# Cross-attention with a feed-forward of three blocks: the norm of the first three token blocks in pieces of its own

## The chip, the cores and the metric

The kernel runs on one core of a Trainium2 chip. The metric is the device time of one execution in microseconds (us); less is better.

Engines: PE (TensorE) multiplies matrices and writes to PSUM; DVE (VectorE), ACT (ScalarE) and POOL (GpSimd) work on vectors, POOL on SBUF alone; SP issues the DMAs. Each engine works through its own instructions in order and waits for others by semaphores.

## What is computed

```python
def xattn(KEY, VALUE, QUERY, ...):              # 128 sequences of 64 tokens, D = 128, 16 heads
    k = split_heads(KEY @ Wk.T + bk); q = split_heads(QUERY @ Wq.T + bq); v = split_heads(VALUE @ Wv.T + bv)
    score = einsum('bhij,bhkj->bhik', k, q) / sqrt(dh)
    attn = softmax(score, axis=1)               # over the heads
    out = einsum('bhik,bhij->bhjk', attn, v)
    return merged(out) @ Wo.T + bo

def ffn(x, ...):                                # weights: 4-bit with scales, plus a low-rank part
    h = x
    for blk in range(3):
        y = qlora_linear(h, 2 * blk)
        y = gelu(layernorm(y, gamma[blk], beta[blk]))
        h = qlora_linear(y, 2 * blk + 1) + h
    return h

x = x + xattn(ctx, ctx, layernorm(x), ...)
x = x + ffn(layernorm(x), ...)
```

## The kernel before

The 8192 tokens are 16 chunks of 512 (four tiles of 128 tokens). The first stage is the attention. Each engine has a function `chunk(c, par, half)`, run for c from 0 to 17, with four parts p from 0 to 3; a part handles 128 tokens (one pair of tiles of scores). In a part, with n = 4c + p:

- PE makes the scores of n + 1, adds the shift by the maximum of n, does a share of the projections for later chunks and of the output projection, and multiplies the probabilities of n - 2 by the values.
- DVE takes the negative maximum over the heads of n (`negmax`, L728), then for n - 1 the sum over the heads (`zsum`, L742) and its reciprocal (`rz`, L745). In part 1 it takes the statistics of a later chunk's x (L524); at the end of part 3 it adds the attention's result to x (`x_all`, L749, semaphore `s_x2`).
- ACT takes the exponential of n (L967) and moves results from PSUM to SBUF.
- POOL multiplies the probabilities of n - 1 by `rz` (L476), and in part 1 works out the variance and scale for x of chunk c + 3 (L439 to L445, L426).

The second stage is the feed-forward, a software pipeline over the 16 blocks of 512 tokens. Each engine has a function `step(t, par)`, in which it does what it has to do for block t in the pipeline's first place, for block t - 1 in its second, and so on over eight places. Block t enters with the layer norm of x: on DVE the statistics of x (`input_stats`, L762) and their combination into mean and variance (`combine_input`, L691 to L703); on POOL the scale by a power of -0.5 (L487), the product with the mean (L502), and the scaling and the shift of x into `z[0]` (L506, L511). PE transposes `z[0]` a step later (semaphore `p_z[0]`), ACT moves it into `h[0]`, and PE's first layer of block t - 2 follows. The combination and the power take the statistics of the new block (the first four columns) and those of the first layer of block t - 2 (the last four) in one instruction each. ACT normalises the first layer (`normalise`, L1021) when the power is there (`p_rs[1]`).

Steps 0 to 4 are issued inside the attention, at the ends of the parts that the table `EARLY` names for each engine as (chunk, part); PE's step 3 stands in part 3 of chunk 15, ahead of that part's output projection, and waits for the last exponential (`s_exp`), since it writes into the PSUM of the scores. Steps from 5 on follow the attention. `s_x2` counts the blocks whose x is complete. The order on each engine is the order in which the program issues the instructions; nothing else plans it.

Within a part the order on DVE is negmax of n, statistics, sum and reciprocal of n - 1, the addition to x, and then early steps; on POOL it is the multiply of n - 1, the variance, and then early steps; on ACT the early step of a part comes after that part's exponential and ahead of the next part's.

Of the kernel before, what the change touches and what calls it, by code (L numbers as in the profile page):

```python
# [19 lines left out]
P = 128  # L20
# [33 lines left out]
         "DVE": {0: (12, 3), 1: (13, 3), 2: (15, 1), 3: (16, 0), 4: (16, 3)},  # L54
         "ACT": {0: (12, 3), 1: (13, 3), 2: (15, 2), 3: (15, 3), 4: (16, 2)},
         "POOL": {0: (12, 3), 1: (13, 3), 2: (15, 1), 3: (16, 0), 4: (16, 2)}}
FIRST_STEP = 5


def build(nc, x, ctx_in, wk, bk, wq, bq, wv, bv, wo, bo, qw, qs, qb, la, lb, gamma, beta, out):  # L60
# [8 lines left out]
    with ExitStack() as es:  # L69
# [6 lines left out]
        def sem(name):  # L76
            return es.enter_context(nc.semaphore(name))
# [150 lines left out]
        p_nmr = sem("p_nmr")  # L228
        p_z0 = sem("p_z0_scaled")
# [26 lines left out]
        def early_steps(eng, c, p, step):  # L256

            if isinstance(c, int):
                for t, place in EARLY[eng].items():
                    if place == (c, p):  # L260
                        step(t, t % 2)

# [153 lines left out]
        def _(pool):  # L416
# [49 lines left out]
            def chunk(c, par, half):  # L466
                for p in range(PPC):
                    n = PPC * c + p
                    mc = c - (p == 0)
                    if live(mc):  # L470
                        m = n - 1

                        pool.wait_ge(s_rz, m + 1)
                        e = probs[(p - 1) % 4]
                        by_query = rz[(p - 1) % 4][:, :].unsqueeze(1).unsqueeze(3)
                        nc.gpsimd.tensor_tensor(e[:, :, :, :], e[:, :, :, :],  # L476
                                                by_query.broadcast_to([P, BANDS, SEQ, ADJ]),
                                                ALU.mult).then_inc(s_probs, 1)
                    if p == 1 and live(c + 3):
                        input_variance(c + 3)  # L480
                    early_steps("POOL", c, p, step)


# [6 lines left out]
            def step(t, par):  # L490
                for v, k in ((3, t - 6), (2, t - 4)):
                    if live(k):
                        if some(k):
                            pool.wait_ge(p_z[v], k)
                        norm_scales(v, 0, TPC, k + 1)
                if live(t) or live(t - 2):
                    if live(t - 3):
                        pool.wait_ge(p_z[1], t - 2)
                    norm_scales(1, 0 if live(t) else TPC, 2 * TPC if live(t - 2) else TPC, t + 1)
                if live(t):  # L500
                    pool.wait_ge(p_rs[1], t + 1)
                    nc.gpsimd.tensor_tensor(nmr2[:, :], nm2[:, :], rs2[1][:, 0:TPC], ALU.mult).then_inc(p_nmr, 1)  # L502

                    if some(t - 1):
                        pool.wait_ge(p_zt[0], t - 1)
                    nc.gpsimd.tensor_tensor(z[0][par][:, :, :], x_all[:, t, :, :],  # L506
                                            rs2[1][:, 0:TPC].unsqueeze(2).broadcast_to([P, TPC, D]),
                                            ALU.mult).then_inc(p_z0, 1)
                    pool.wait_ge(p_nmr, t + 1)
                    pool.wait_ge(p_z0, t + 1)  # L510
                    nc.gpsimd.tensor_tensor(z[0][par][:, :, :], z[0][par][:, :, :],  # L511
                                            nmr2[:, :].unsqueeze(2).broadcast_to([P, TPC, D]),
                                            ALU.add).then_inc(p_z[0], 1)
# [7 lines left out]
        def _(dve):  # L521
# [162 lines left out]

            def combine_input(k, lo, hi):

                st, ag = st2[1][:, lo:hi, :], ag2[1][:, :, lo:hi]
                dve.wait_ge(p_bn[1], k + 1)
                if some(k):
                    dve.wait_ge(p_rs[1], k)  # L690
# [4 lines left out]
                dve.wait_ge(p_mv[1], 2 * k + 1)  # L695
                if lo == 0:
                    if some(k):
                        dve.wait_ge(p_nmr, k)
# [3 lines left out]
                dve.wait_ge(p_mv[1], 2 * k + 2)  # L702
# [17 lines left out]
            def chunk(c, par, half):  # L720
                for p in range(PPC):
# [48 lines left out]
            def step(t, par):  # L770
# [18 lines left out]
                if live(t) or live(t - 2):  # L789
                    combine_input(t, 0 if live(t) else TPC, 2 * TPC if live(t - 2) else TPC)  # L790
# [23 lines left out]
        def _(act):  # L814
# [210 lines left out]
            def step(t, par):  # L1025
# [34 lines left out]
                if live(t - 2):  # L1060
                    normalise(1, t - 2, TPC, t + 1, first_layer_bank(1, t, par))
# [403 lines left out]
```

## Time and profile before

| | us |
|---|---|
| median of 3 runs | 375.77 (375.29 to 377.1) |
| the profiled execution | 373.36 |
| its span | 371.6 |

| engine | busy us | share of the span |
|---|---|---|
| PE | 340.4 | 92% |
| DVE | 333.2 | 90% |
| ACT | 285.5 | 77% |
| POOL | 268.6 | 72% |

The span is the time from the first to the last recorded instruction of the profiled execution; the rest of its 373.36 us lies around it. In a timeline row the first number is the start in us from the span's beginning, the second the length, then engine, line and operation, output and inputs with their shapes, and how many instructions are merged; idle time of the engine ahead of it stands in brackets with what ended it. The chain is the work that ended last, followed back from the last instruction. Attention with its early steps runs until about 247 us, the feed-forward alone from there on. The granted clock of TensorE has the mean 0.994.

### The profile page before, as it was taken

The numbers are of one execution on the slowest core, as the hardware profiler recorded it, in microseconds if no ns is written. First come the engines' busy times: TensorE is split into PE (matmuls) and PEld (weight loads), VectorE is DVE, ScalarE is ACT, GpSimd is POOL, SyncE is SP. The second block draws the span as 40 slices with busy tenths as digits, with TensorE's granted clock in tenths as the row PEclk, the third lists the DMA queues.
The fourth block names the chain that finished last, engine by engine and source line by source line (L and its number), as shares of the span: only waits on it lengthen the run. The fifth ranks groups of instructions, "written<-read, shape, count | busy, mean of one in ns | idle before, by whom it ended". The sixth has DMA issues, their size and how long they took to land.

```text
span 371.6 us, 13058 instructions
## 1 busy us (share of the span) xinstructions
PE 340.4 (92%) x4795; PEld 253.4 (68%) x4795; DVE 333.2 (90%) x832; ACT 285.5 (77%) x572; POOL 268.6 (72%) x265
## 2 busy tenths in 40 slices
PE   7777999999999999999979785988999999999983
PEld 5443566677667766776756563775888888888773
DVE  5869999999999999999999999879999999988752
ACT  4585988778888878887867545558899999999862
POOL 4546698788877987788788878867878787873321
PEclk9899999999999999999999999999999999999999
DMA  8784475567548645854661400000010001110112
GB/s 197 217 272 148 143 236 179 157 201 223 174 134 232 202 153 152 254 182 145 185 198 63 140 4 2 3 0 1 2 59 29 28 28 56 31 31 30 57 47 67
DMA packets 54498, 43.29 MB, mean 117 GB/s; under 512 B 4592, under 2 KB 48576, under 8 KB 54464
## 3 DMA queue, kind: packets, MB, share of 16 engines
q1 hardware_dynamic: 53888, 42.31, 37.9%
q10 hardware_dynamic: 576, 0.53, 0.5%
q8 instruction: 21, 0.34, 0.4%
q14 instruction: 13, 0.11, 0.1%
HBM read 26.05 MB, written 16.78 MB: 115 GB/s over the span
## 4 chain that ended last, share of the span: by engine, by line
PE 63%; DVE 23%; issue 6%; ACT 4%; POOL 3%; POOLq 0%; DVEq 0%; ACTq 0%
PE score_ps L1367 10%; DVE negmax L728 7%; DVE zsum L742 7%; PE att_ps L1343 6%; PE score_ps L1281 5%; PE wo_ps L1125 5%; PE work L1428 3%; PE score_ps L1137 3%; PE score_ps L1435 3%; PE work L1161 3%; PE att_ps L1435 3%; PE score_ps L1361 3%; PE work L1167 3%; PE work L1174 2%; DVE st L767 2%
## 5 line engine op out<-in xcount | busy, mean ns | idle before, releaser
L476 POOL TENSOR_TENSOR probs<-probs,rz 128x1024 f32<-128x1024 f32 x64 | 136.3, 2139 | 35.7 <-DVE rz L745 35.5
L487 POOL TENSOR_TENSOR rs<-ve,minus_half 128x4 f32<-128x4 f32 (+1 forms) x50 | 59.3, 1187 | 41.5 <-DVE ve L682 30.1
L967 ACT ACTIVATE probs<-score_ps 128x1024 f32<-128x1024 f32 x64 | 65.7, 1026 | 24.7 <-PE score_ps L1281 24.3
L742 DVE TENSOR_REDUCE zsum<-probs 128x64 f32<-128x1024 f32 x64 | 77.3, 1208 | 0.8 <-ACT probs L967 0.8
L728 DVE TENSOR_REDUCE negmax<-score_ps 128x64 bf16<-128x1024 f32 x64 | 75.2, 1176 | 0.3 <-PE score_ps L1137 0.3
L1021 ACT ACTIVATE z<-score_ps,rs 128x128 f32<-128x128 f32 x160 | 46.0, 383 | 2.6 <-POOL rs L487 2.6
L1367 PEld LDWEIGHTS score_ps<-lin_t,h 128*128 128x128 f32 x320 | 38.9, 191 | 12.1 <-DVE h L805 7.0
L1281 PE MATMUL score_ps<-negmax,ident_bf 128*128 128x512 bf16 x128 | 38.8, 384 | 9.2 <-DVE negmax L728 9.1
L1125 PEld LDWEIGHTS wo_ps<-wo_t,att_t 128*128 128x128 f32 x256 | 36.8, 191 | 13.7 <-issue 12.1
L1367 PE MATMUL score_ps<-lin_t,h 128*128 128x128 f32 x320 | 42.0, 278 | 3.0 <-ACT probs L967 1.1
L1343 PE MATMUL att_ps<-probs,v_diag 128*32 128x64 f32 x2048 | 43.4, 224 | 1.5 <-POOL probs L476 0.7
L1343 PEld LDWEIGHTS att_ps<-probs,v_diag 128*32 128x32 f32 x2048 | 32.8, 108 | 11.4 <-POOL probs L476 3.2
L767 DVE BATCH_NORM_STATS2 st<-score_ps 128x6 f32<-128x128 f32 x160 | 35.6, 286 | 4.2 <-PE score_ps L1367 3.2
L1125 PE MATMUL wo_ps<-wo_t,att_t 128*128 128x128 f32 x256 | 38.2, 275 | 0.0
L745 DVE RECIPROCAL rz<-zsum 128x64 f32<-128x64 f32 x64 | 35.4, 553 | 2.2
L1137 PE MATMUL score_ps<-q_stack,k_stack 64*64 64x128 f16 x1024 | 26.7, 222 | 1.1 <-ACT probs L967 0.5
L1137 PEld LDWEIGHTS score_ps<-q_stack,k_stack 64*64 64x64 f16 x1024 | 16.7, 106 | 12.5 <-issue 11.2
L426 POOL TENSOR_TENSOR half_rstd<-veps,minus_half 128x4 f32<-128x4 f32 x16 | 16.3, 1018 | 11.0 <-DVE veps L536 10.0
L1031 ACT ACTIVATE g<-score_ps,cols 128x512 f32<-128x512 f32 x25 | 19.9, 798 | 5.4 <-PE score_ps L1361 5.4
L1428 PEld LDWEIGHTS work<-lin_t,g 128*128 128x128 f32 x128 | 16.6, 191 | 8.0 <-issue 6.7
L834 ACT ACTIVATE xln<-x_all,half_rstd 128x128 f32 (+1 forms) x60 | 19.1, 393 | 0.4 <-POOL half_rstd L426 0.4
L886 ACT ACTIVATE v_diag<-work 64x512 f32<-64x512 f32 x32 | 18.8, 588 | 0.4
(192 smaller groups left out, 669.7 us busy)
## 6 DMA issues: line engine op xcount, KB each, us to landing
q_parts<-parts SPq DMA_DIRECT2D x15, 512.0 KB, 3.5
k_stack<-k_parts SPq DMA_DIRECT2D x30, 256.0 KB, 3.3
q_stack<-q_parts SPq DMA_DIRECT2D x60, 128.0 KB, 2.9
ctx_sb<-in_ctx SPq DMA_DIRECT2D x16, 256.0 KB, 3.6
k_parts<-parts SPq DMA_DIRECT2D x16, 256.0 KB, 2.8
out<-x_all SPq DMA_DIRECT2D x16, 256.0 KB, 2.3
x_all<-in_x SPq DMA_DIRECT2D x14, 256.0 KB, 3.8
x_all<-in_x SPq DMA_DIRECT2D x1, 512.0 KB, 5.5
```

The lines of the kernel that those rows point to most:

```text
L476: nc.gpsimd.tensor_tensor(e[:, :, :, :], e[:, :, :, :], by_query.broadcast_to([P, BANDS, SEQ, ADJ]), ALU.mult).then_inc(s_probs, 1)
L487: nc.gpsimd.tensor_tensor(rs2[v][:, lo:hi], ve2[v][:, lo:hi], minus_half[:, lo:hi], ALU.pow).then_inc(p_rs[v], 1)
L728: nc.vector.tensor_reduce(negmax[p % 2][:, :], score_ps[p % 2][:, :].rearrange("p (h k) -> p k h", k=SEQ), AX_X, ALU.max, negate=True).the ...
L742: nc.vector.tensor_reduce(zsum[q][:, :], probs[(p - 1) % 4][:, :, :, :].rearrange("p u k s -> p k u s"), AX_XY, ALU.add).then_inc(s_zsum, 1)
L767: ins = nc.vector.bn_stats(st2[v][:, lo + i, :], src[:, TILE * i:TILE * (i + 1)])
L967: nc.scalar.activation(probs[p][:, :, :, :], score_ps[p % 2][:, :].rearrange("p (u s k) -> p u k s", s=ADJ, k=SEQ), ACT.Exp, scale=SCALE). ...
L1021: ins = nc.scalar.activation(z[v][0][:, t, :], src[:, TILE * t:TILE * (t + 1)], ACT.Copy, scale=rs2[v][:, lo + t:lo + t + 1])
L1125: ins = nc.tensor.matmul(wo_ps[:, TILE * t:TILE * (t + 1)], att[:, o, TILE * u:TILE * (u + 1)], wo_t[:, o, b, :], start=False, stop=o == 1 ...
L1137: ins = nc.tensor.matmul(score_ps[mp % 2][SEQ * b:SEQ * (b + 1), c0:c0 + 2 * SEQ], k_stack[mb][half_rows, grp, k0:k0 + SEQ], q_stack[mb][h ...
L1281: ins = nc.tensor.matmul(score_ps[p % 2][:, CHUNK * o:CHUNK * (o + 1)], ident_bf[:, :], negmax[p % 2][:, :].unsqueeze(1).broadcast_to([P, ...
L1343: ins = nc.tensor.matmul(att_ps[32 * grp:32 * (grp + 1), c0:c0 + SEQ], v_diag[mb][:, v0:v0 + 32], probs[mp][:, band(hd), :, hd % ADJ], sta ...
L1367: ins = nc.tensor.matmul(dst[:, TILE * t:TILE * (t + 1)], hk[:, TILE * t:TILE * (t + 1)], lin_t[:, 2 * v - 2, :], start=v == 1 and t == 0, ...
```

## The change

The norm of x for blocks 0, 1 and 2 is taken out of the steps and cut into five pieces, each with a table of places in chunks 12 to 15: statistics and combination on DVE, scale (with the product), scaling and shift on POOL. They have semaphores of their own (`p_xbn`, `p_xmv`, `p_xst`, `p_xrs`). Steps 0 and 1 are gone from DVE and POOL, and step 0 from ACT, since nothing else was in them. Step 2 keeps what it does for the first layer of block 0; on POOL it moves from (15, 1) to (15, 2). Blocks from 3 on are as before, with counts that start later.

```diff
 EARLY = {"PE": {0: (12, 3), 1: (13, 3), 2: (15, 0), 4: (16, 2)},
-         "DVE": {0: (12, 3), 1: (13, 3), 2: (15, 1), 3: (16, 0), 4: (16, 3)},
-         "ACT": {0: (12, 3), 1: (13, 3), 2: (15, 2), 3: (15, 3), 4: (16, 2)},
-         "POOL": {0: (12, 3), 1: (13, 3), 2: (15, 1), 3: (16, 0), 4: (16, 2)}}
+         "DVE": {2: (15, 1), 3: (16, 0), 4: (16, 3)},
+         "ACT": {1: (13, 3), 2: (15, 2), 3: (15, 3), 4: (16, 2)},
+         "POOL": {2: (15, 2), 3: (16, 0), 4: (16, 2)}}
 FIRST_STEP = 5
+
+AHEAD = 3
+X_STATS = {0: (12, 0), 1: (13, 0), 2: (14, 0)}
+X_COMBINE = {0: (12, 2), 1: (13, 2), 2: (14, 2)}
+X_SCALES = {0: (12, 3), 1: (13, 3), 2: (14, 3)}
+X_SCALED = {0: (13, 0), 1: (14, 0), 2: (15, 0)}
+X_SHIFTED = {0: (13, 2), 1: (14, 1), 2: (15, 1)}
...
+        def later(t):
+
+            return not isinstance(t, int) or AHEAD <= t < NCHUNK
...
                     if p == 1 and live(c + 3):
                         input_variance(c + 3)
+                    input_part(X_SCALES, c, p, input_scales)
+                    input_part(X_SCALED, c, p, input_scaled)
+                    input_part(X_SHIFTED, c, p, input_shifted)
                     early_steps("POOL", c, p, step)
 
+            def input_scales(t):
+                pool.wait_ge(p_xst, t + 1)
+                nc.gpsimd.tensor_tensor(rs2[1][:, 0:TPC], ve2[1][:, 0:TPC], minus_half[:, 0:TPC],
+                                        ALU.pow).then_inc(p_xrs, 1)
+                pool.wait_ge(p_xrs, t + 1)
+                input_offset(t)
...
-                if live(t) or live(t - 2):
+                own = later(t)
+                if own or live(t - 2):
                     if live(t - 3):
                         pool.wait_ge(p_z[1], t - 2)
-                    norm_scales(1, 0 if live(t) else TPC, 2 * TPC if live(t - 2) else TPC, t + 1)
-                if live(t):
-                    pool.wait_ge(p_rs[1], t + 1)
...
+                    norm_scales(1, 0 if own else TPC, 2 * TPC if live(t - 2) else TPC, t - 1)
+                if own:
+                    pool.wait_ge(p_rs[1], t - 1)
+                    input_offset(t)
+                    input_scaled(t, par)
+                    input_shifted(t, par)
...
+            def input_stats_ahead(t):
+                dve.wait_ge(s_x2, t + 1)
+                if t > 0:
+                    dve.wait_ge(p_xst, t)
+                input_stats(t).then_inc(p_xbn, 1)
+
+            def combine_ahead(t):
+                st, ag = st2[1][:, 0:TPC, :], ag2[1][:, :, 0:TPC]
+                dve.wait_ge(p_xbn, t + 1)
+                nc.vector.scalar_tensor_tensor(ag[:, 1, :], st[:, :, 2], EPS * D, st[:, :, 5], ALU.add, ALU.add)
+                nc.vector.tensor_tensor(ag[:, 0, :], st[:, :, 1], st[:, :, 4], ALU.add)
+                nc.vector.tensor_tensor(ag[:, 2, :], st[:, :, 1], st[:, :, 4], ALU.subtract).then_inc(p_xmv, 1)
+                dve.wait_ge(p_xmv, 2 * t + 1)
+                if t > 0:
+                    dve.wait_ge(p_nmr, t)
+                nc.vector.tensor_scalar(nm2[:, :], ag[:, 0, :], -0.5, None, ALU.mult)
+                nc.vector.scalar_tensor_tensor(ag[:, 3, :], ag[:, 2, :], 0.25, ag[:, 2, :], ALU.mult,
+                                               ALU.mult).then_inc(p_xmv, 1)
+                dve.wait_ge(p_xmv, 2 * t + 2)
+                nc.vector.scalar_tensor_tensor(ve2[1][:, 0:TPC], ag[:, 1, :], 1.0 / D, ag[:, 3, :], ALU.mult,
+                                               ALU.add).then_inc(p_xst, 1)
...
+                    input_part(X_STATS, c, p, input_stats_ahead)
+                    input_part(X_COMBINE, c, p, combine_ahead)
                     early_steps("DVE", c, p, step)
...
-                if live(t) and isinstance(t, int) and t <= FIRST_STEP:
-                    ins = input_stats(t)
-                    if t < 2:
-                        ins.then_inc(p_bn[1], 1)
+                if isinstance(t, int) and AHEAD <= t <= FIRST_STEP:
+                    input_stats(t)
...
-                if live(t) or live(t - 2):
-                    combine_input(t, 0 if live(t) else TPC, 2 * TPC if live(t - 2) else TPC)
+                if live(t - 2):
+                    combine_input(t, 0 if later(t) else TPC, 2 * TPC)
...
                 if live(t - 2):
-                    normalise(1, t - 2, TPC, t + 1, first_layer_bank(1, t, par))
+                    normalise(1, t - 2, TPC, t - 1, first_layer_bank(1, t, par))
```

`input_scaled` and `input_shifted` hold the two instructions of L506 and L511 with their waits, `input_offset` that of L502, and `input_part` issues a piece at the place in its table.

## Rows read from the trace of the kernel before

**Rows 1.** Busy time in a stretch: us, then each engine, clock, DMA share, GB/s.

```profile
176.58:226.59 50.01, 43.32 (x890) 31.41 (x888) 49.21 (x84) 31.80 (x48) 40.71 (x30) 1.00 0.35 109
```

**Rows 2.** The chain in order of time (start, length, what), chunk 15's end.

```profile
229.45 1.17 DVE negmax L728
...
231.31 1.03 ACT probs L967
...
232.39 1.16 PE score_ps L1367 x8
```

**Rows 3.** Timeline of DVE, chunk 12 and step 0.

```profile
180.50 0.86 DVE L524 BATCH_NORM_STATS2 stats<-x_all 128x6 f32<-128x128 f32 x4
181.27 1.21 DVE L742 TENSOR_REDUCE zsum<-probs 128x64 f32<-128x1024 f32 x1
...
189.14 0.86 DVE L762 BATCH_NORM_STATS2 st<-x_all 128x6 f32<-128x128 f32 x4
190.04 1.69 DVE L691 SCALAR_TENSOR_TENSOR ag<-st 128x4 f32<-128x4 f32 x1
191.65 0.15 DVE L693 TENSOR_TENSOR ag<-st 128x4 f32<-128x4 f32 x1
...
192.26 1.22 DVE L728 TENSOR_REDUCE negmax<-score_ps 128x64 bf16<-128x1024 f32 x1
```

**Rows 4.** Timeline of POOL, chunks 12 to 15.

```profile
183.14 2.14 POOL L476 TENSOR_TENSOR probs<-probs,rz 128x1024 f32<-128x1024 f32 x1 [1.41 <-DVE rz L745]
...
187.48 4.23 POOL L476 TENSOR_TENSOR probs<-probs,rz 128x1024 f32<-128x1024 f32 x2
...
193.66 1.04 POOL L506 TENSOR_TENSOR z<-x_all,rs 128x512 f32<-128x512 f32 x1
194.84 1.04 POOL L511 TENSOR_TENSOR z<-z,nmr 128x512 f32<-128x512 f32 x1
...
200.85 2.13 POOL L476 TENSOR_TENSOR probs<-probs,rz 128x1024 f32<-128x1024 f32 x1 [0.65 <-DVE rz L745]
203.64 2.14 POOL L476 TENSOR_TENSOR probs<-probs,rz 128x1024 f32<-128x1024 f32 x1 [0.65 <-DVE rz L745]
...
223.88 2.13 POOL L476 TENSOR_TENSOR probs<-probs,rz 128x1024 f32<-128x1024 f32 x1 [0.65 <-DVE rz L745]
226.75 1.65 POOL L487 TENSOR_TENSOR rs<-ve,minus_half 128x8 f32<-128x8 f32 x1 [0.74 <-DVE ve L703]
```

**Rows 5.** Timeline of DVE, steps 1 and 2.

```profile
200.69 1.16 DVE L728 TENSOR_REDUCE negmax<-score_ps 128x64 bf16<-128x1024 f32 x1
...
204.02 0.86 DVE L762 BATCH_NORM_STATS2 st<-x_all 128x6 f32<-128x128 f32 x4
204.91 0.89 DVE L691 SCALAR_TENSOR_TENSOR ag<-st 128x4 f32<-128x4 f32 x1
...
206.34 1.22 DVE L728 TENSOR_REDUCE negmax<-score_ps 128x64 bf16<-128x1024 f32 x1
...
223.72 0.81 DVE L762 BATCH_NORM_STATS2 st<-x_all 128x6 f32<-128x128 f32 x4
...
225.36 0.69 DVE L691 SCALAR_TENSOR_TENSOR ag<-st 128x8 f32<-128x8 f32 x1
...
226.59 1.22 DVE L728 TENSOR_REDUCE negmax<-score_ps 128x64 bf16<-128x1024 f32 x1
```

**Rows 6.** Timeline of ACT, step 2: the first layer of block 0 normalised.

```profile
230.01 1.15 ACT L1021 ACTIVATE z<-work,rs 128x128 f32<-128x128 f32 x4
```

**Rows 7.** Timelines of POOL and DVE in the feed-forward: a power and a combine.

```profile
256.06 1.02 POOL L487 TENSOR_TENSOR rs<-ve,minus_half 128x4 f32<-128x4 f32 x1 [0.38 <-DVE ve L682]
...
256.82 0.17 DVE L679 SCALAR_TENSOR_TENSOR ag<-st 128x4 f32<-128x4 f32 x1
```

**Rows 8.** POOL's memsets by line (min/median/max ns); DVE's timeline beside the longest.

```profile
L452 POOL MEMSET v_diag<- x8: 519/524/1206, 16.9 to 23.0; 128x512 f32 x8
...
17.64 0.53 DVE L622 TENSOR_SCALAR w_deq<-qw_in 128x768 f32<-128x768 int32 x1
```

More of the change, by code:

```diff
@@ L261, in early_steps, with input_part @@
                         step(t, t % 2)
+        def input_part(places, c, p, part):
+            if isinstance(c, int):
+                for t, place in places.items():
+                    if place == (c, p):
+                        part(t)
+        def later(t):
+            return not isinstance(t, int) or AHEAD <= t < NCHUNK
         def chunks(eng, body):
@@ L480, in chunk, with input_offset, input_scaled, input_shifted @@
                         input_variance(c + 3)
+                    input_part(X_SCALES, c, p, input_scales)
+                    input_part(X_SCALED, c, p, input_scaled)
+                    input_part(X_SHIFTED, c, p, input_shifted)
                     early_steps("POOL", c, p, step)
+            def input_scales(t):
[4 more added lines that the diff above has]
+                input_offset(t)
+            def input_offset(t):
+                nc.gpsimd.tensor_tensor(nmr2[:, :], nm2[:, :], rs2[1][:, 0:TPC], ALU.mult).then_inc(p_nmr, 1)
+            def input_scaled(t, par=None):
+                if some(t - 1):
+                    pool.wait_ge(p_zt[0], t - 1)
+                nc.gpsimd.tensor_tensor(z[0][t % 2 if par is None else par][:, :, :], x_all[:, t, :, :],
+                                        rs2[1][:, 0:TPC].unsqueeze(2).broadcast_to([P, TPC, D]),
+                                        ALU.mult).then_inc(p_z0, 1)
+            def input_shifted(t, par=None):
+                zt = z[0][t % 2 if par is None else par][:, :, :]
+                pool.wait_ge(p_nmr, t + 1)
+                pool.wait_ge(p_z0, t + 1)
+                nc.gpsimd.tensor_tensor(zt, zt, nmr2[:, :].unsqueeze(2).broadcast_to([P, TPC, D]),
+                                        ALU.add).then_inc(p_z[0], 1)
             def norm_scales(v, lo, hi, count):
@@ L683, in combine_layer @@
                                                ALU.add).then_inc(p_st[v], 1)
+            def input_stats_ahead(t):
[18 more added lines that the diff above has]
+                                               ALU.add).then_inc(p_xst, 1)
             def combine_input(k, lo, hi):
                 st, ag = st2[1][:, lo:hi, :], ag2[1][:, :, lo:hi]
-                dve.wait_ge(p_bn[1], k + 1)
-                if some(k):
-                    dve.wait_ge(p_rs[1], k)
+                dve.wait_ge(p_bn[1], k - 1)
+                if some(k - 2):
+                    dve.wait_ge(p_rs[1], k - 2)
                 nc.vector.scalar_tensor_tensor(ag[:, 1, :], st[:, :, 2], EPS * D, st[:, :, 5], ALU.add, ALU.add)
@@ L694, in combine_input @@
                 nc.vector.tensor_tensor(ag[:, 2, :], st[:, :, 1], st[:, :, 4], ALU.subtract).then_inc(p_mv[1], 1)
-                dve.wait_ge(p_mv[1], 2 * k + 1)
+                dve.wait_ge(p_mv[1], 2 * k - 3)
                 if lo == 0:
-                    if some(k):
-                        dve.wait_ge(p_nmr, k)
+                    dve.wait_ge(p_nmr, k)
                     nc.vector.tensor_scalar(nm2[:, :], ag[:, 0, 0:TPC], -0.5, None, ALU.mult)
```

14 lines of the change are left out of this document (2 added, 12 removed).

## The prediction

> **What bounds the kernel now.** The places that the change touches lie in chunks 12 to 15, so I read the busy time of that stretch first [rows 1]. From the first negmax of chunk 12 to the third of chunk 15 VectorE (DVE) is busy 49.21 of 50.01 us; PE has 43.32, ACT 31.80, GpSimd (POOL) 40.71. Next the chain in order of time [rows 2]: through this stretch it runs on DVE alone (negmax, sum, reciprocal, part after part), leaves it at the last negmax of chunk 15 (229.45), and goes over PE's shift to ACT's last exponential (231.31) and PE's step 3 (232.39). Two things follow. Until 229.45 a microsecond of DVE more or less is a microsecond of the end. At 231.31 the engine to watch is ACT: what delays the last exponential delays everything, because step 3 on PE waits for it and all later PE work stands behind step 3.
>
> Then the timelines of DVE and POOL side by side. At the end of chunk 12 the first instruction of the combine (L691, `ag<-st`, two inputs in SBUF) takes 1.69 us on 4 columns [rows 3]; the same kind of instruction elsewhere takes 0.17 [rows 7]. It ends at 191.73, when POOL's two multiplies of probs (187.48 + 4.23 = 191.71) end [rows 4]. At step 1 it takes 0.89 and ends at 205.80, POOL's multiply at 205.78; at step 2 it takes 0.69 and ends at 226.05, the multiply at 226.01 [rows 4, 5]. Three of three: a DVE instruction with two SBUF inputs waits until the POOL multiply that is under way is done. These waits are 1.52, 0.72 and 0.52 us, together 2.76, and lie on the chain.
>
> **What the change removes from DVE.** Step 0 (189.14 to 192.26, 3.12 us), step 1 (204.02 to 206.34, 2.32) and step 2 (223.72 to 226.59, 2.87), in all 8.31 us, waits included [rows 3, 5].
>
> **What it adds to DVE.** Three times four statistics after parts (12,0), (13,0), (14,0): 0.77 each by the same instruction on x in chunk 12 (180.50 to 181.27), 2.31. Three combines after (12,2), (13,2), (14,2): without a wait 0.71 each (0.61 from the second instruction to the next negmax, 191.65 to 192.26, and some 0.10 for the first), 2.13 [rows 3]. Step 2 keeps the statistics of the first layer (223.72 to 225.36 less 0.77, 0.87) and four of the six combine instructions, an estimated 0.53 as two of the six (0.08 to 0.09 each) go: 1.40 [rows 5]. Sum 5.84. So the third negmax of chunk 15, at 226.59 before, comes 8.31 - 5.84 = 2.47 us earlier, plus the waits for POOL at the new places. Stats lose nothing: one SBUF input, and the old ones ran beside POOL's work at their normal length.
>
> **The waits at the new places.** All three combines now stand right behind a reciprocal, and that reciprocal is what POOL's multiply waits for: DVE's next instruction began at 200.69, the multiply at 200.85, 0.16 us later [rows 4, 5]. The six instructions come as three, a semaphore, two, a semaphore, one. The multiply (2.14 us) thus arrives among them.
> - Chunk 12: POOL is in the variance of chunk 15 then (its next multiply waits from 183.14 + 2.1 to 187.48 behind six small instructions and moves with the statistics added) [rows 4]. Bounds 0 and 0.5 us, taken 0.2, since the small instructions are short and the power doesn't hold DVE up: L679 ran 0.17 us at 256.82 in the middle of a power from 256.06 to 257.08 [rows 7].
> - Chunk 13: DVE's first three get through (0.33 us), the other three stand behind the multiply until about 2.3 us after the combine's start: 2.05 us. `input_shifted` of block 0 (1.04 us, as the row at 194.84) follows the multiply without a gap, and DVE's last instruction, behind its own semaphore, may meet it too: 2.75. Taken 2.4. Lower bound 0, if DVE is through before the multiply reads.
> - Chunk 14: a multiply and the shift of block 1 take 2.14 + 1.04 = 3.18 us, more than a part of DVE (226.59 to 229.45, 2.86), so the shift is still running when the combine starts, by some 0.55 us; the next multiply follows at once. 0.55 + 2.05 = 2.6, lower bound 0.55.
> - Step 2 in (15,1): its combine starts 0.9 us after the reciprocal. POOL has scale 2 (a power, 1.02 [rows 7], and a small product) and scaled 2 (1.04) in the parts before and begins its multiply some 0.5 us late; the wait is 1.8, or 2.8 with the shift of block 2 behind it. Taken 2.3 [rows 4].
>
> Sum 0.2 + 2.4 + 2.6 + 2.3 = 7.5 us in place of a gain: the third negmax of chunk 15 comes 7.5 - 2.47 = 5.0 us later.
>
> The Trainium skill, "SBUF — State Buffer", section "Who interferes with whom", states the rule behind these waits and speaks against the change: a DVE instruction with two SBUF inputs contends with a GpSimd instruction that reads SBUF, one of them blocks fully for the other's whole length, and issue order decides which. It counts `tensor_scalar` in its two-port mode in too, which no row here shows. The multiply's rows agree; the power's row (0.17 us beside a power of 1.02) doesn't. Taken to the letter for the power, chunk 12's combine could wait 1 us more, and the sum would be 6.0 instead of 5.0.
>
> **The wait that is new on ACT.** POOL's step 2 moves from (15,1) to (15,2), behind that part's multiply, while ACT's step 2 stays at (15,2), ahead of the last exponential. It normalises block 0 and needs POOL's power. Before, the power started at 226.75, 0.16 us after the negmax behind the combine [rows 4, 5], and ACT normalised from 230.01 to 231.16 without waiting for it [rows 6]. Now the multiply waits for the reciprocal of (15,2), 2.94 us behind the negmax at S (part 2.86 [rows 2, 5] and 0.08); multiply at S + 3.0 to 5.15, power 1.02 [rows 7] to S + 6.1, normalise 1.15 to S + 7.3, and only then the last exponential. Before, it began at 231.31 = S + 4.72 [rows 2]. That is 2.6 us. Queued behind the waiting instruction are that exponential and, through it, PE's step 3, the output projection of chunk 14 and DVE's last sum. Nothing covers it: the exponential is on the chain.
>
> **The rest.** POOL's pieces replace the same instructions and POOL waits less, but it isn't on the chain. PE's transposes of blocks 0, 1 and 2 find them ready: shift 0 ends 1.04 us after a multiply that ended at 202.98 [rows 4], while PE used it first after the end of chunk 13. ACT's other steps and SP's queue are untouched; no DMA moves. Behind step 3 the order is as before and PE is next in line, so I let nothing be won back.
>
> Sum: + 5.0 + 2.6 = + 7.6 us. The profiled run took 373.36 us (span 371.6 and 1.8 around it), 2.4 below the median of 375.77; a shift of this stretch carries over unchanged, so 375.77 + 7.6 = 383.4.
>
> **Rivals.**
> 1. DVE keeps the port through its six instructions, and waits only where POOL is already reading. For: the longest memset of POOL, 1206 ns against 524, ran while DVE's L622 began, so POOL too can be the one that waits [rows 8]. Against: between DVE's groups stand two semaphores. Waits 0.2 + 0 + 0.55 + 1.8 = 2.55, + 0.1 + 2.6: 378.5.
> 2. Not slower: DVE isn't held up at any of the four places, the mechanism of rival 1 to its end, with POOL's reads always coming last. Price - 2.47 + 0.2 + 2.6 = + 0.3: 376.1. It decides if the six are through before the multiply's first read, that is if this comes over 0.6 us after its start. Against it: the three waits of before.
> 3. The wait of ACT lies beside another wait of the same length (PE's step 3 held by something else), the port as in the forecast: + 5.0, 380.8. Nothing in the chain shows such a wait.
> 4. Faster: rivals 2 and 3 together, - 2.3: 373.5.
> 5. The change doesn't do what it says: the pieces relieve nobody, since POOL's waits in steps 0 and 1 are off the chain and DVE has the same instructions elsewhere. With no other wait that ends at rival 2's time.
>
> **How the numbers follow.** Forecast 0.58 (its own range, by the bounds of the waits, 382.0 to 385.2), rival 1 0.19, rivals 2 and 5 0.11, rival 3 0.06, rival 4 0.06. A measurement of this kernel can tell about 0.5%, 1.9 us, from no change: below 373.9 lies rival 4 (0.06), between 373.9 and 377.7 rivals 2 and 5 and a little of rival 1 (0.13), above it the rest (0.81). The range for 8 in 10 must take in rival 1: 377.4 to 385.2.
>
> **What will show it.** Right: in the combines ahead of (13,3) and (14,3) one instruction of 2 us that ends with a POOL multiply; a gap on ACT ahead of the normalise of block 0, released by POOL's power; the last exponential about 7 us later. Wrong: combine instructions of 0.17 us throughout with multiplies that start later or last longer (rivals 1, 2), or an exponential that is late while PE's step 3 isn't (rival 3).

## The result and the profile after

| | median of 4 runs, us | lowest to highest |
|---|---|---|
| before, on the same chip | 376.44 | 375.29 to 378.37 |
| after | 384.75 | 384.14 to 386.73 |

The ratio is 1.0225 with the interval 1.0188 to 1.0262: the change makes the kernel slower by 8.3 us, where 7.6 were forecast. The profiled execution of after took 385.16 us (span 383.4). That of before, 373.36 us, is among the fastest that before has: its mean granted clock was 0.994, and of the 41 other executions of before that stand beside the experiments one has 0.994 (373.29 us) and forty have 0.976 to 0.990 (373.45 to 378.48 us). Ratios and medians are of the fast runs alone, those within 1.5% of a kernel's fastest; this leaves out three of the ten runs of experiment 3 (380.38 to 381.83 us; its median with them is 377.73) and one of the twelve of experiment 8 (552.79 us at a mean clock of 0.559; with it 371.78).

The stretch of [rows 1], from the first negmax of chunk 12 to the third of chunk 15, is now 55.03 us long instead of 50.01, and DVE is busy in 53.88 of it (us; PE, weight loads, DVE, ACT, POOL; granted clock; DMA share; GB/s):

```profile
179.21:234.24 55.03, 45.11 (x890) 32.79 (x888) 53.88 (x89) 31.75 (x48) 43.77 (x34) 0.97 0.31 99
```

What it is busy with are the combines. They stand in the timeline of DVE of after (start, length, engine, line, operation; L732 to L742 are the combine ahead of its step, L751 to L762 that of step 2, L787 the negmax behind it), in chunks 12, 13, 14 and in step 2:

```profile
189.17 0.10 DVE L732 SCALAR_TENSOR_TENSOR ag<-st 128x4 f32<-128x4 f32 x1
...
189.81 1.23 DVE L787 TENSOR_REDUCE negmax<-score_ps 128x64 bf16<-128x1024 f32 x1
...
202.39 0.10 DVE L732 SCALAR_TENSOR_TENSOR ag<-st 128x4 f32<-128x4 f32 x1
...
202.67 2.04 DVE L738 TENSOR_SCALAR nm<-ag 128x4 f32<-128x4 f32 x1
204.63 0.15 DVE L739 SCALAR_TENSOR_TENSOR ag<-ag 128x4 f32<-128x4 f32 x1
204.81 0.89 DVE L742 SCALAR_TENSOR_TENSOR ve<-ag 128x4 f32<-128x4 f32 x1
205.62 1.21 DVE L787 TENSOR_REDUCE negmax<-score_ps 128x64 bf16<-128x1024 f32 x1
...
218.20 0.53 DVE L732 SCALAR_TENSOR_TENSOR ag<-st 128x4 f32<-128x4 f32 x1
...
218.73 2.08 DVE L734 TENSOR_TENSOR ag<-st 128x4 f32<-128x4 f32 x1
...
221.20 1.23 DVE L787 TENSOR_REDUCE negmax<-score_ps 128x64 bf16<-128x1024 f32 x1
...
231.65 1.47 DVE L751 SCALAR_TENSOR_TENSOR ag<-st 128x4 f32<-128x4 f32 x1
...
233.23 0.89 DVE L759 SCALAR_TENSOR_TENSOR ag<-ag 128x4 f32<-128x4 f32 x1
...
234.24 1.22 DVE L787 TENSOR_REDUCE negmax<-score_ps 128x64 bf16<-128x1024 f32 x1
```

And POOL at the same times, with its multiply (L495), its shift of x (L527) and its power (L533):

```profile
202.56 2.13 POOL L495 TENSOR_TENSOR probs<-probs,rz 128x1024 f32<-128x1024 f32 x1 [0.64 <-DVE rz L804]
204.65 1.04 POOL L527 TENSOR_TENSOR z<-z,nmr 128x512 f32<-128x512 f32 x1
...
217.67 1.04 POOL L527 TENSOR_TENSOR z<-z,nmr 128x512 f32<-128x512 f32 x1
218.67 2.13 POOL L495 TENSOR_TENSOR probs<-probs,rz 128x1024 f32<-128x1024 f32 x1
...
230.96 2.15 POOL L495 TENSOR_TENSOR probs<-probs,rz 128x1024 f32<-128x1024 f32 x1 [0.21 <-DVE rz L804]
233.05 1.05 POOL L527 TENSOR_TENSOR z<-z,nmr 128x512 f32<-128x512 f32 x1
237.25 2.12 POOL L495 TENSOR_TENSOR probs<-probs,rz 128x1024 f32<-128x1024 f32 x1 [3.15 <-DVE rz L804]
239.34 1.01 POOL L533 TENSOR_TENSOR rs<-ve,minus_half 128x4 f32<-128x4 f32 x1
```

These answer [rows 3 to 5]. Each long DVE instruction on four columns ends with a POOL instruction: L738 at 204.71 with the multiply that ends at 204.69, L742 at 205.70 with the shift that ends at 205.69, L734 at 220.81 with the multiply that ends at 220.80. A combine without a wait takes 0.64 us (chunk 12, 189.17 to 189.81). What the others take beyond that is their wait: 3.23 - 0.64 = 2.59 us in chunk 13 and 3.00 - 0.64 = 2.36 in chunk 14. Step 2's four instructions take 2.59 instead of the estimated 0.53: 2.06. Together 7.0. In what follows, "the port" is short for what these rows show: one of the two engines, DVE with its operands in SBUF or POOL, stands until the other's instruction is done.

Next ACT at the end of chunk 15, which answers [rows 6] and the exponential of [rows 2] (L1080 normalises block 0, L1026 is the exponential):

```profile
236.16 1.02 ACT L1026 ACTIVATE probs<-score_ps 128x1024 f32<-128x1024 f32 x1 [3.02 <-PE score_ps L1340]
...
240.39 1.14 ACT L1080 ACTIVATE z<-work,rs 128x128 f32<-128x128 f32 x4 [2.62 <-POOL rs L533]
241.40 1.04 ACT L1026 ACTIVATE probs<-score_ps 128x1024 f32<-128x1024 f32 x1
```

ACT stands still for 2.62 us until POOL's power is through, and the last exponential comes behind it. The chain of waits of after shows the same (start, length, what):

```profile
237.25 2.12 POOL probs L495
239.38 0.98 POOL rs L533
...
241.53 0.92 ACT probs L1026
...
242.49 2.07 PE score_ps L1426 x8
```

Its last line was not foreseen. Before, these matmuls of step 3 took 1.16 us [rows 2]. PE's timeline and the busy time by stretch of after:

```profile
235.52 0.60 PE L1340 MATMUL score_ps<-negmax,ident_bf 128*128 128x512 bf16 x2 [2.47 <-DVE negmax L787]
...
242.49 2.07 PE L1426 MATMUL score_ps<-lin_t,h 128*128 128x128 f32 x8 [3.15 <-ACT probs L1026]
244.36 1.06 PE L1420 MATMUL score_ps<-ident,z 128*128 128x128 f32 x4
```

```profile
218.80:222.48 3.68, 0.02 (x4) 0.01 (x1) 3.61 (x7) 0.00 (x0) 1.99 (x1) 1.00 0.00 0
222.48:227.00 4.52, 4.52 (x48) 3.73 (x48) 4.45 (x6) 2.21 (x3) 2.78 (x2) 0.62 0.00 0
234.24:242.49 8.25, 3.03 (x40) 1.62 (x40) 6.22 (x9) 3.69 (x8) 5.19 (x3) 0.64 0.01 2
242.49:247.60 5.11, 5.09 (x19) 4.06 (x20) 4.52 (x16) 2.52 (x3) 2.44 (x2) 0.57 0.00 2
```

and the stretches of before from its third negmax of chunk 15 to its last exponential, and of step 3:

```profile
226.59:231.31 4.72, 2.26 (x40) 1.34 (x40) 4.68 (x6) 2.64 (x6) 4.33 (x5) 1.00 0.01 3
232.39:236.00 3.61, 3.18 (x19) 2.37 (x20) 3.58 (x11) 2.52 (x3) 3.61 (x3) 1.00 0.00 0
```

Before, step 3 had the clock at 1.00. After, PE was busy for 3.03 of the 8.25 us ahead of step 3, the granted clock fell to a mean of 0.64, and step 3 ran at 0.57, most of it at the lower of the two levels (1.2 of 2.4 GHz). Cut into half microseconds, the clock is 1.00 until 236.5 and 0.50 from 237.0 to 246.5. So it fell a good microsecond after PE had come back from a pause of 2.47 us (233.05 to 235.52), and before ACT's wait for POOL began (237.76). The same happened once more, in chunk 15: PE idled 3.66 us behind chunk 14's combine, and the clock of the 4.5 us after that was 0.62.

For the comparison of kernels I cut the profiled executions at four rows that each of them has: DVE's addition to x of block 9 (the end of chunk 11), the third negmax of chunk 15 (S), the start of the last exponential, and DVE's addition of block 15. A, B and C are the stretches between them. This leaves out the start of the kernel: there after took 2.6 us more than before (from its third negmax to its fourth 7.20 us, 4.69 before), with the same instructions. The traces of the experiments show either length: this first row lies at 175.77 to 176.03 in before and experiments 2 and 4, at 177.60 to 179.82 in the others. In after the clock of that stretch (28.2 to 33.3) was 0.67, before's 1.00, and a DVE tensor_scalar on two columns (L705, 36.37 to 37.41) stood behind a POOL multiply (35.26 to 37.38).

| kernel | A: to S | B: S to the last exponential | C: to the last addition | sum |
|---|---|---|---|---|
| before | 176.03 to 226.59: 50.56 | to 231.31: 4.72 | to 246.50: 15.19 | 70.47 |
| after | 178.66 to 234.24: 55.58 | to 241.40: 7.16 | to 258.04: 16.64 | 79.38 |
| difference | +5.02 | +2.44 | +1.45 | +8.91 |

The profiled difference of 8.91 us in the stretch stands beside 8.31 by the medians; the whole profiled executions differ by 11.8. Since before's profile has a higher clock than nearly all its other executions, C's +1.45 is measured against a good case of before, and is likely less against its median execution.

### The profile page after: what moved, and what is told of

Its sections match the earlier page's. It is cut to its first block, busy times and chain, and to the rows that moved or that the text cites. A ratio compares the mean times of both kernels' runs of the same rounds, so it can differ in the third digit from the quotient of the medians.

```text
span 383.4 us, 13055 instructions
## 1 busy us (share of the span) xinstructions
PE 346.6 (90%) x4795; PEld 257.9 (67%) x4795; DVE 338.4 (88%) x836; ACT 284.7 (74%) x572; POOL 268.5 (70%) x266
## 4 chain that ended last, share of the span: by engine, by line
PE 64%; DVE 22%; issue 5%; POOL 4%; ACT 4%; POOLq 0%; DVEq 0%; ACTq 0%
PE score_ps L1426 10%; PE att_ps L1402 6%; DVE zsum L801 6%; PE score_ps L1340 6%; DVE negmax L787 5%; PE wo_ps L1184 5%; PE score_ps L1196 3%; PE work L1487 3%; PE score_ps L1494 3%; PE work L1220 3%; PE att_ps L1494 3%; PE score_ps L1420 3%; PE work L1226 3%; PE work L1233 3%; POOL probs L495 2%
## 5 line engine op out<-in xcount | busy, mean ns | idle before, releaser
L495 POOL TENSOR_TENSOR probs<-probs,rz 128x1024 f32<-128x1024 f32 x64 | 136.3, 2138 | 47.3 <-DVE rz L804 47.3
L1026 ACT ACTIVATE probs<-score_ps 128x1024 f32<-128x1024 f32 x64 | 65.6, 1025 | 29.1 <-PE score_ps L1340 28.7
L533 POOL TENSOR_TENSOR rs<-ve,minus_half 128x4 f32<-128x4 f32 (+1 forms) x48 | 56.6, 1180 | 42.0 <-DVE ve L720 32.8
L787 DVE TENSOR_REDUCE negmax<-score_ps 128x64 bf16<-128x1024 f32 x64 | 75.6, 1181 | 0.0
L1340 PE MATMUL score_ps<-negmax,ident_bf 128*128 128x512 bf16 x128 | 39.6, 392 | 11.9 <-DVE negmax L787 11.8
L1080 ACT ACTIVATE z<-score_ps,rs 128x128 f32<-128x128 f32 x160 | 45.8, 382 | 2.4 <-POOL rs L533 2.4
L1426 PE MATMUL score_ps<-lin_t,h 128*128 128x128 f32 x320 | 42.9, 282 | 5.1 <-ACT probs L1026 3.1
L1340 PEld LDWEIGHTS score_ps<-negmax,ident_bf 128*128 128x128 bf16 x128 | 7.3, 97 | 18.4 <-DVE negmax L787 13.4
```

What stands on the lines that cost most here:

```text
L495: nc.gpsimd.tensor_tensor(e[:, :, :, :], e[:, :, :, :], by_query.broadcast_to([P, BANDS, SEQ, ADJ]), ALU.mult).then_inc(s_probs, 1)
L533: nc.gpsimd.tensor_tensor(rs2[v][:, lo:hi], ve2[v][:, lo:hi], minus_half[:, lo:hi], ALU.pow).then_inc(p_rs[v], 1)
L787: nc.vector.tensor_reduce(negmax[p % 2][:, :], score_ps[p % 2][:, :].rearrange("p (h k) -> p k h", k=SEQ), AX_X, ALU.max, negate=True).the ...
L1026: nc.scalar.activation(probs[p][:, :, :, :], score_ps[p % 2][:, :].rearrange("p (u s k) -> p u k s", s=ADJ, k=SEQ), ACT.Exp, scale=SCALE). ...
L1080: ins = nc.scalar.activation(z[v][0][:, t, :], src[:, TILE * t:TILE * (t + 1)], ACT.Copy, scale=rs2[v][:, lo + t:lo + t + 1])
L1340: ins = nc.tensor.matmul(score_ps[p % 2][:, CHUNK * o:CHUNK * (o + 1)], ident_bf[:, :], negmax[p % 2][:, :].unsqueeze(1).broadcast_to([P, ...
```

## The experiments

The theory: A's excess is DVE behind POOL at the port, B's is POOL's power behind a multiply, and C's is the clock, which falls because PE is lightly busy while A and B last. The rivals: A is mere length (DVE has its instructions in worse places), B's exponential is late for another reason, and the clock falls whatever ACT waits for. The results in one table, with the cuts of above; ratios are to before's runs on the same chip (medians 375.7 beside the first four, 376.9 beside five and six, 376.56 beside the last two) and are not quotients of the medians. A to C come from one trace each:

| kernel | A | B | C | sum | median us | ratio (interval) |
|---|---|---|---|---|---|---|
| 1 after, POOL's step 2 early | 56.92 | 4.72 | 16.16 | 77.80 | 382.92 | 1.0182 (1.0096 to 1.0269) |
| 2 after, combine ahead of rz | 50.83 | 7.18 | 17.24 | 75.25 | 380.22 | 1.0149 (1.0065 to 1.0233) |
| 3 both | 51.26 | 4.72 | 16.16 | 72.14 | 376.95 | 1.0019 (0.9967 to 1.0071) |
| 4 before, POOL's step 2 late | 51.84 | 7.80 | 16.62 | 76.26 | 380.55 | 1.0151 (1.0069 to 1.0233) |
| 5 = 3, no waits for the port | 47.83 | 4.64 | 16.19 | 68.66 | 373.82 | 0.9897 (0.9847 to 0.9948) |
| 6 after, 70 matmuls of zeros | 56.09 | 7.18 | 17.88 | 81.15 | 383.96 | 1.0194 (1.0140 to 1.0248) |
| 7 after, 38 matmuls of zeros | 55.44 | 7.17 | 15.01 | 77.62 | 381.37 | 1.0133 (1.0061 to 1.0204) |
| 8 = 5, 16 matmuls of zeros | 47.84 | 4.64 | 15.28 | 67.76 | 371.25 | 0.9881 (0.9843 to 0.9920) |

### 1. POOL's step 2 back where it was

```diff
-         "POOL": {2: (15, 2), 3: (16, 0), 4: (16, 2)}}
+         "POOL": {2: (15, 1), 3: (16, 0), 4: (16, 2)}}
```

> The changed kernel with one entry put back: POOL's step 2 at (15,1) instead of (15,2). My theory (the new wait on ACT is real and on the chain): POOL's power of step 2 starts within 0.3 us of DVE's combine, ACT normalises block 0 without a wait, the last exponential starts 4.7 us after the third negmax of chunk 15 instead of 7.2; PE stands idle ahead of its step 3 for about 1 us instead of 3.15, so its clock stays at 2.4 GHz and the matmuls of step 3 take 1.16 us instead of 2.07. The four waits of DVE for POOL stay (about 7 us). Time about 4 us under the changed kernel's 384.75: 380.7, ratio to before 1.011. Rival (the wait lies beside another of the same length): 384.7, ratio 1.022. Rival (the wait goes, but the clock falls all the same): 382.3.

B is 4.72 again, to the hundredth that of before, and ACT's last exponential waits for PE's shift and no longer for POOL. But step 3 isn't at full clock (timelines of ACT and PE, then its stretch):

```profile
241.46 1.02 ACT L1026 ACTIVATE probs<-score_ps 128x1024 f32<-128x1024 f32 x1 [0.16 <-PE score_ps L1340]
...
242.53 1.45 PE L1426 MATMUL score_ps<-lin_t,h 128*128 128x128 f32 x8 [1.11 <-ACT probs L1026]
```

```profile
242.50:247.30 4.80, 4.75 (x19) 3.53 (x20) 4.70 (x16) 2.55 (x3) 4.26 (x2) 0.64 0.00 0
```

The wait of ACT is shown as the cause of B, whole. Of C only 0.48 us came back, and the median, 382.92, lies by the case in which the clock falls all the same. The 2.44 us of ACT's wait are therefore not needed for it to fall. A was 1.34 us longer than after's, 0.87 of it in chunk 15 and 0.49 in chunk 14: PE's clock was low for longer there and DVE waited for it. The gain stands on the rows more than on the medians: the interval of the ratio overlaps that of after.

### 2. The combine ahead of the reciprocal

```diff
                                                 AX_XY, ALU.add).then_inc(s_zsum, 1)
+                        input_part(X_COMBINE, c, p, combine_ahead)
                         dve.wait_ge(s_zsum, m + 1)
                         nc.vector.reciprocal(rz[(p - 1) % 4][:, :], zsum[q][:, :]).then_inc(s_rz, 1)
...
-                    input_part(X_COMBINE, c, p, combine_ahead)
```

The six instructions are the same; only the one that releases POOL's multiply now comes after them.

> The changed kernel with the three combines put between DVE's sum and its reciprocal instead of behind the reciprocal, so that POOL's multiply, which waits for that reciprocal, can't start among their six instructions. My theory (a DVE instruction with its operands in SBUF stands behind a POOL instruction that is under way): the wait in chunk 13 (2.59 us) goes to under 0.1, the one in chunk 14 falls from 2.36 to about 1.0, since the shift of block 1 is still running there, step 2 keeps its 2.1, ACT keeps its wait and PE its low clock at step 3. About 4.3 us under the changed kernel: 380.4, ratio 1.011. Rival (the waits only move to POOL, which then makes DVE or PE late elsewhere): 384, ratio 1.02. Rival (the instruction is slow for another reason than POOL, as its place behind a reciprocal): the same 2 us instructions at the new place in both chunks or in neither.

DVE's timeline, chunks 13 and 14 and step 2:

```profile
199.27 0.17 DVE L738 TENSOR_SCALAR nm<-ag 128x4 f32<-128x4 f32 x1
...
212.08 1.04 DVE L733 TENSOR_TENSOR ag<-st 128x4 f32<-128x4 f32 x1
...
223.85 1.78 DVE L751 SCALAR_TENSOR_TENSOR ag<-st 128x4 f32<-128x4 f32 x1
...
225.74 0.89 DVE L759 SCALAR_TENSOR_TENSOR ag<-ag 128x4 f32<-128x4 f32 x1
```

L738 takes 0.17 us where it took 2.04. In chunk 14 what is left is the shift of block 1, which waits for no reciprocal (212.07 to 213.10 on POOL); step 2 was not moved and waits as before. A falls by 4.75 us, B is as in after. So A is the port, and the place of six small instructions by half a microsecond decides over some 4 us. That A was mere length is refuted: the same instructions are there. So is that a place behind a reciprocal makes them slow: chunk 12's combine stood behind one in after and took 0.64 us, and L733 here stands ahead of one and took 1.04. The intervals of the two ratios just overlap, but every run (379.41 to 382.23 us) is below after's fastest (384.14).

### 3. Both

> Both edits together: combines ahead of the reciprocal, POOL's step 2 at (15,1). If the two causes are separate and both on the chain, their gains add: 384.75 - 4.0 - 4.3 = 376.4, ratio to before 1.000. If they share time (one is hidden when the other is gone), clearly less than the sum: 379 or more.

376.95 (376.4 were expected if the gains add), ratio 1.0019: the change as it stands with these two edits undoes the loss, to what can be told. In the stretch the gains were 1.58 and 4.13 alone and 7.24 together; 0.91 us of the 1.53 beyond the sum of the two is in A, where experiment 1 had met the low clock for longer, the rest in C.

### 4. The kernel before with one entry moved

```diff
-         "POOL": {0: (12, 3), 1: (13, 3), 2: (15, 1), 3: (16, 0), 4: (16, 2)}}
+         "POOL": {0: (12, 3), 1: (13, 3), 2: (15, 2), 3: (16, 0), 4: (16, 2)}}
```

> The kernel before with one entry changed: POOL's step 2 at (15,2) instead of (15,1), nothing else. It does the one part of the change alone. There the step also holds block 2's own norm, so the power has 8 columns (1.65 us). My theory: the last exponential starts about 3 us later behind the third negmax of chunk 15 than before (4.72), and PE idles long enough ahead of step 3 for its clock to fall: 3 to 5 us over before, 379.5 to 381.5, ratio 1.008 to 1.013. Rival (hidden): 376.4, ratio 1.000.

Timelines of ACT and PE, and the stretch of step 3:

```profile
234.40 1.14 ACT L1021 ACTIVATE z<-work,rs 128x128 f32<-128x128 f32 x4 [3.26 <-POOL rs L487]
...
236.50 2.07 PE L1367 MATMUL score_ps<-lin_t,h 128*128 128x128 f32 x8 [4.21 <-ACT probs L967]
```

```profile
236.40:241.70 5.30, 5.18 (x19) 4.17 (x20) 5.02 (x16) 2.60 (x4) 4.58 (x3) 0.58 0.01 2
```

This is ACT's wait alone, with nothing of the five pieces: B +3.08 (POOL's power is here on eight columns and takes 1.65 us, not 1.01), and C +1.43 at a clock of 0.58. One entry in a table costs 4.85 us by the medians. A was also longer by 1.28 us; it lies in chunk 13, where the instructions are those of before and DVE waited for ACT and PE at a lower clock:

```profile
190.00:204.00 14.00, 11.94 (x227) 8.05 (x225) 12.88 (x17) 8.38 (x15) 11.04 (x8) 0.88 0.36 114
```

Before had 1.00 there. Why it fell in this execution and not in that of before is open.

### 5. No wait for the port at all

Experiment 3 with DVE's step 2 moved ahead of the reciprocal of (15, 1), the shift of block 1 a part later, and POOL's shifts behind its early steps:

```diff
-         "DVE": {2: (15, 1), 3: (16, 0), 4: (16, 3)},
+         "DVE": {3: (16, 0), 4: (16, 3)},
...
-X_SHIFTED = {0: (13, 2), 1: (14, 1), 2: (15, 1)}
+X_SHIFTED = {0: (13, 2), 1: (14, 2), 2: (15, 1)}
...
-                    input_part(X_SHIFTED, c, p, input_shifted)
                     early_steps("POOL", c, p, step)
+                    input_part(X_SHIFTED, c, p, input_shifted)
...
                         input_part(X_COMBINE, c, p, combine_ahead)
+                        if isinstance(c, int) and (c, p) == (15, 1):
+                            step(2, 0)
```

> Both edits and three more places: DVE's step 2 ahead of the reciprocal of (15,1), the shift of block 1 at (14,2) instead of (14,1), and the shift of block 2 behind POOL's step 2 in (15,1). With this no DVE combine in chunks 12 to 15 should meet POOL at work. My theory: the first instructions of all four combines take 0.17 us or at most 0.35, against 7.0 us of waits in the changed kernel, 3.1 in the kernel with both edits and 2.76 in the kernel before. By the sum, 2.9 us under the kernel with both edits: 374.8 if PE's clock still falls at step 3, about 373 if it doesn't; ratio to before (375.7) 0.992 to 0.998. Rival (a part of the wait is only moved, to POOL and from there to ACT's normalise): ACT waits up to 1 us for POOL's power and the time stays at 376 to 377.

The longest wait that is left is that of step 2's first instruction, and the end of step 3 is still at the low clock (timelines of DVE and PE):

```profile
225.36 0.45 DVE L751 SCALAR_TENSOR_TENSOR ag<-st 128x4 f32<-128x4 f32 x1
...
235.25 1.90 PE L1496 MATMUL work<-g,lin_t 128*128 128x512 f32 x2
```

A holds the same instructions as after's and is 2.73 us shorter than before's: that is what the pieces are worth without the waits. It is nearly the 2.76 us of before's own three waits. So the gain is that DVE no longer meets POOL, not less work, and no run shows whether before's combines, moved ahead of a reciprocal, would gain the same. The median, 373.82, lies between the two that were expected; the ratio, 1.0% below before's, is lower than the expected 0.992, and step 2's first instruction at 0.45 us is above the expected 0.35. But the clock falls although neither DVE nor ACT waits any more (C 16.19). The waits of the change aren't needed for that, nor a long pause: PE's pauses from S to step 3 were 0.83, 0.97 and 1.11 us here, and the clock fell within step 3; in before they were 2.16, 1.14 and 1.11, and it stayed at 1.00.

### 6 and 7. The clock alone

Matmuls of zeros are added into sums that are open in PSUM, which changes no value: in experiment 6, 24 in part (14, 3), 16 in (15, 2), 6 in (15, 3) and 24 ahead of step 3; in experiment 7, 14, 9, 3 and 12 in the same places. No wait is touched.

```diff
+            def add_zeros(count, dst):
+                for i in range(count):
+                    nc.tensor.matmul(dst[:, 0:P], ident[:, :], zeros[:, :], start=False, stop=False,
+                                     skip_group_check=True)
...
+                        add_zeros({(14, 3): 24, (15, 2): 16, (15, 3): 6}.get((c, p), 0), wo_ps if p == 2 else att_ps)
...
+                        add_zeros(24, att_ps)
                         step(3, 1)
```

> The changed kernel with 70 matmuls of zeros added into open sums on PE, at the places in chunks 14 and 15 where PE stands idle for 3.66, 2.47, 0.80 and 3.15 us; nothing waits for them and the result stays the same. It asks whether PE's idle time ahead of step 3 is what lowers its clock there. If so, the matmuls of step 3 take 1.16, 0.60, 0.60 us again instead of 2.07, 1.06, 1.06, and those of the value projection in chunk 14 1.05 instead of 1.91; the chain then loses 0.9 + 0.85 + 0.3 us at step 3 and 0.4 in chunk 15: 382.3, against 384.75. Rival (the matmuls are slow there for a reason of their own): 384.7 and the same lengths. Rival (the zeros delay PE): above 385.

> The changed kernel with zeros on PE as in the run before it, but half as many (38): there each f32 matmul of zeros took 0.22 us, so 24 of them ran 2.1 and 3.0 us past the waits that they were to fill. With 14, 9, 3 and 12 they take 3.1, 2.0, 0.7 and 2.7 us where PE stood idle for 3.66, 2.47, 0.80 and 3.15, so nothing is delayed. My theory (the low clock at step 3 and in the value projection of chunk 14 follows from PE's idle time and costs 2.0 and 0.4 us): step 3 at 1.16, 0.60, 0.60, 382.3 against 384.75, ratio to before 1.014. Rival (what the clock costs at step 3 is covered by a later wait): the matmuls are short, but the time stays at 384 or more.

PE's timeline in experiment 6, then in experiment 7, and the stretches of 7 from 0.9 us behind S to step 3 and of step 3:

```profile
240.59 5.52 PE L1259 MATMUL att_ps<-zeros,ident 128*128 128x128 f32 x48
245.94 1.06 PE L1437 MATMUL score_ps<-lin_t,h 128*128 128x128 f32 x8
```

```profile
241.35 1.16 PE L1437 MATMUL score_ps<-lin_t,h 128*128 128x128 f32 x8 [0.91 <-ACT probs L1028]
```

```profile
234.00:241.35 7.35, 5.80 (x70) 4.92 (x70) 5.30 (x8) 3.69 (x8) 5.21 (x3) 1.00 0.00 0
241.35:245.50 4.15, 3.71 (x23) 2.79 (x23) 4.08 (x13) 2.52 (x3) 2.13 (x1) 1.00 0.02 4
```

In 6 step 3's matmuls run at full rate, but the zeros last 3.0 us beyond the end of the exponential (242.92), and step 3 starts behind them at 245.94: the gain is eaten, and 383.96 misses what was expected. With fewer of them PE is busy 5.80 of 7.35 us, the clock stays at 1.00 in both stretches, step 3's first matmuls take 1.16 us and C is 15.01, 1.63 less than in after. A and B are as in after, and the median falls to 381.37; every run (379.90 to 383.38 us) is below after's fastest, on another chip, while the intervals of the two ratios overlap. So C in after was the clock, and in this kernel work for PE in the waits held it.

### 8. No waits, and the clock held

Experiment 5 with 4, 3, 4 and 5 matmuls of zeros in the same places.

> The kernel without port waits (373.8) with 16 matmuls of zeros where PE still waits for 0.8 to 1.2 us in chunks 14 and 15 and ahead of step 3. There its clock still fell within step 3 (1.00, 1.06, 1.90 us instead of 0.60, 0.60, 1.13). If idle time is the cause, step 3 runs at full rate and 1.6 us are won: 372.2, ratio to before 0.986. Rival (the clock falls there anyway, since PE's work is light on both sides): 373.8.

```profile
231.16 1.16 PE L1439 MATMUL score_ps<-lin_t,h 128*128 128x128 f32 x8
...
228.00:236.00 8.00, 7.57 (x108) 6.01 (x96) 7.89 (x17) 5.51 (x10) 7.99 (x5) 1.00 0.00 0
```

The clock holds (first line: timeline; second: stretch), C falls by 0.91, and the kernel is the fastest of all: 371.25 (372.2 were expected), 1.2% less than before by the ratio. Its interval overlaps that of experiment 5, so that the zeros add anything here rests on C and the rows, not on the medians. Before was not run with matmuls of zeros, so it is open what they alone would bring there.

## Why the prediction was right, step by step

- **The bound.** DVE until late in chunk 15, then ACT's last exponential: the chain of after runs that way, except that it leaves DVE at the reciprocal of (15,2), ahead of the fourth negmax, and goes over POOL's multiply and power. Where the clock is low it also runs over PE (222.48 to 228.01). Experiment 1 took away ACT's wait alone, experiment 2 most of DVE's alone.
- **Removed less added, -2.47 us.** It can be read only where no wait hides it: A of experiment 5 is 2.73 shorter than before's. Of the 8.31 us removed 2.76 were waits, so the work itself was forecast to grow, from 5.55 to 5.84 us; the prediction has them as "waits included" and doesn't say that. The 0.53 us for step 2's four instructions is met there (225.36 to 226.20, 0.84, of which the first instruction waited 0.30).
- **The waits for POOL, 7.5 us forecast, 7.0 measured.** Chunk 12: 0.2, measured 0; the six ran beside POOL's small variance instructions at 0.10 to 0.17 each. Chunk 13: 2.4, measured 2.59, split as said into an instruction of 2 us behind the multiply and one behind the shift. Chunk 14: 2.6, measured 2.36 (0.55 + 2.05 became 0.53 and 2.08 in length). Step 2: 2.3, measured 2.06, but split otherwise: the multiply was not half a microsecond late (it began 0.64 us behind the start of its reciprocal, as in chunk 13), and L751 waited 1.32 for it and L759 0.73 for the shift. The first three instructions passed in chunk 13, as forecast. In chunk 14 the first waited for the shift, the second passed, and the third met the multiply.
- **The third negmax of chunk 15, +5.0.** A is +5.02, but by terms: -2.47 + 7.0 is 4.5. Of the other 0.5, 0.36 is DVE waiting until 229.07 for an exponential that PE's low clock had made late; the rest isn't traced. The agreement to 0.02 is in part luck, small errors that cancel.
- **ACT's wait, +2.6.** Measured +2.44, and without the pieces, in experiment 4, +3.08.
- **"I let nothing be won back"** is the step that was mis-sized. The prediction put it at nothing. The part behind the last exponential was not unchanged but 1.45 us longer (C). Step 3's instructions were costed as if their length were fixed; in after they ran at little more than half the rate, after a stretch in which PE was lightly busy. Experiments 6 and 7 show the rate, and that more work for PE ahead held it; that it is the change's waits that lower the clock isn't shown, since it fell in experiments 1, 3 and 5 too, where C is 16.16 to 16.19. That before keeps it at step 3 is seen in one profile, with a mean clock (0.994) that nearly all its other executions stay below; what they have at step 3 is open. The 8.91 us of the stretch are 5.02 + 2.44 + 1.45, and the prediction had the first two.
- **The range.** The forecast's own range, 382.0 to 385.2 "by the bounds of the waits", doesn't come out of these bounds: 0 + 0 + 0.55 + 1.8 gives 378.3, and 0.5 + 2.75 + 2.6 + 2.8 gives 384.6. The measured 384.75 lies just above the latter; it holds what C added.
- **The rivals.** Rivals 1, 2 and 5 (DVE keeps the port) fall by the rows L738, L734 and L751, and by experiment 2, where the waits go with their cause; rival 5's time, 376.1, isn't met either. Rival 3 (ACT's wait lies beside another) falls by B in experiments 1 and 4, and with it rival 4.
- **The page.** The Trainium skill, "SBUF — State Buffer", section "Who interferes with whom", says that `tensor_scalar` can contend, in its two-port modes; none of the prediction's rows showed that. The row of after agrees: L738, one input in SBUF and four columns, took 2.04 us beside a multiply, and L705 at the kernel's start 1.04, where before's took 0.17 with no multiply beside it. The page's rule taken to the letter for small instructions of POOL shows no wait here: chunk 12's combine took 0.64 us in all beside instructions of POOL that last 0.2 us each by their records; for how much of that they read SBUF no row shows.

## What to carry to other kernels

Before a DVE step of small instructions is moved, look which POOL instruction the DVE instruction ahead of it releases: put the small ones ahead of the release, not behind it. A piece of a step that another engine waits for in order (here ACT for POOL's power) belongs ahead of POOL's long instruction; one entry in a table cost 4.85 us. And the end of a stage can cost more than the waits ahead of it: where PE is lightly busy, read the granted clock of the stretch behind, and count the matmuls there at the rate of the rows that have that clock. One profile of the kernel before can be a good case: compare its mean clock with that of the other executions.

## What was not expected of the hardware

- The clock fell while PE was at work, about 1.1 us behind the end of a pause: in after, with 3.03 of 8.25 us busy and pauses of 2.47, 0.80 and 3.15 us, it went from 1.00 to the low level behind the first of them, and eight matmuls took 2.07 us instead of 1.16. In experiment 5 it fell with no pause above 1.11 us behind S. With 5.80 of 7.35 us busy, part of it zeros, it stayed at 1.00.
- In these rows the port is won anew for each DVE instruction. In chunk 13 three instructions went through, the last of them (L734, 202.48 to 202.64) while the multiply was already recorded as begun (202.56); the next, L738, from 202.67, stood behind it for 2 us. In chunk 14 of experiment 2 only the second of six waited.
- With the same instructions, the granted clock differed between executions in places that no edit touched (1.00 and 0.88 in the profiles of before and of experiment 4, around chunk 13). What decides it is open; it goes with the time: before's executions with a mean clock of 0.988 or more took 373.29 to 375.94 us, those with 0.982 or less 376.56 to 378.48.
